# A four-stage graph network: one normalisation written with a stride-zero tensor operand, and the turn of the gated layers' state one step later

## The reference

```
layer 0 (attention and feed-forward, inner part)
  scores = sum(q[src] * k[dst]) / sqrt(16) + edge_attr @ eW + eb
  attn   = softmax of the scores over the edges of one dst
  out    = segment_sum(v[src] * attn, dst) @ oW + ob
  x1     = layer_norm(x + out) * g1 + b1
  h      = gelu(layer_norm(x1 @ f1W + f1b) * gf + bf) @ f2W + f2b
  return layer_norm(x1 + h) * g2 + b2
layer 1: mean of the neighbours, two 128x128 products, L2 norm
layer 2: h = x @ lin_w.T + lin_b; three times
  agg = segment_sum((h @ weight[i])[src], dst)
  r = sigmoid(W_ir agg + W_hr h + b);  z = sigmoid(W_iz agg + W_hz h + b)
  n = tanh(W_in agg + b_in + r * (W_hn h + b_hn))
  h = (1 - z) * n + z * h
layer 3: concat(x, mean of the neighbours) @ weight
```

## Time and profile before

| what | us |
|---|---|
| median of the runs (3) | 6054.59 |
| lowest and highest run | 6049.87, 6078.45 |
| profiled execution | 6070.21 |
| its span | 6068.3 |

### The profile page before, as it was taken

How to read it: one execution, slowest core, us unless ns; L and a number is a source line. 1 busy time by engine, 2 the same in 40 slices (tenths; PEclk the granted TensorE clock), 3 DMA queues, 4 the chain that set the end, 5 groups by cost and what they waited for, 6 DMA issues and landing times. The chain is left out here.

```text
span 6068.3 us, 76920 instructions
## 1 busy us (share of the span) xinstructions
PE 4367.1 (72%) x16790; PEld 2619.4 (43%) x16790; DVE 4101.2 (68%) x13622; ACT 2768.2 (46%) x6238; POOL 3623.7 (60%) x3234
## 2 busy tenths in 40 slices
PE   6688859999998565545666579977896669936643
PEld 3355544444444333334444344534443334436643
DVE  6566658999998544447776576557665889836633
ACT  0233326777776010136666345534443446536643
POOL 4665638888886788845555661046204757855455
PEclk8787769999999777778888899989998889968876
DMA  6222223333332343356665575457544667757621
GB/s 213 62 76 72 73 66 88 99 100 98 98 98 75 74 62 62 59 102 198 187 199 181 169 210 161 131 150 216 172 141 141 176 161 204 202 163 226 190 78 54
DMA packets 767746, 802.51 MB, mean 132 GB/s; under 512 B 139776, under 2 KB 527944, under 8 KB 767162
## 3 DMA queue, kind: packets, MB, share of 16 engines
q1 hardware_dynamic: 405498, 393.44, 22.9%
q0 software_dynamic: 117504, 209.42, 14.6%
q10 hardware_dynamic: 244288, 194.72, 9.6%
HBM read 445.32 MB, written 351.92 MB: 131 GB/s over the span
## 5 line engine op out<-in xcount | busy, mean ns | idle before, releaser
L462 PE MATMUL gate_bank<-gate_ht,gate_whh 128*128 128x512 f32 x1764 | 872.4, 618 | 28.6 <-DVE gate_n L532 15.8
L925 POOL DMA_INDIRECT xh<-mean_xh,mean_pos_all x392 | 378.4, 965 | 338.9 <-DVE mean_xh L1027 142.2
L462 PEld LDWEIGHTS gate_bank<-gate_ht,gate_whh 128*128 128x128 f32 x1764 | 341.8, 202 | 407.0 <-issue 384.7
L2080 PE MATMUL back_ps_sums<-back_same,back_rows 128*128 128x512 f32 x400 | 286.6, 883 | 291.5 <-DMA back_rows<-x_a,back_idx 291.5
L151 POOL DMA_INDIRECT ffn_rows<-att_sums,ffn_idx x392 | 409.6, 1045 | 114.8 <-issue 106.3
L289 POOL DMA_INDIRECT gate_rows<-h_a,by_pos x200 | 197.8, 989 | 429.0 <-POOLq L117 328.4
L1521 PE MATMUL ffn_ps_f<-ffn_hg,ffn_f 128*128 128x512 f32 x784 | 407.1, 616 | 47.6 <-ACT ffn_hg L1698 47.6
L458 PE MATMUL gate_bank<-by_rank,gate_win 128*128 128x512 f32 x882 | 436.0, 594 | 0.0
L1514 PE MATMUL ffn_ps_u<-ffn_xs_t,ffn_up_w 128*128 128x512 f32 x784 | 387.0, 596 | 1.1 <-issue 1.1
L2061 POOL DMA_INDIRECT back<-back_out,back_dest x200 | 324.1, 1620 | 67.8 <-issue 60.1
L583 ACT ACTIVATE gate_z<-gate_bank,gate_b_rz 128x512 f32<-128x512 f32 x294 | 201.5, 685 | 346.0 <-PE gate_bank L462 225.6
(11 more groups left out here) (273 smaller groups left out, 12080.1 us busy)
## 6 DMA issues: line engine op xcount, KB each, us to landing
mean_x<-x_a SPq DMA_DIRECT2D x196, 256.0 KB
back<-blank ACTq DMA_DIRECT2D x99, 264.0 KB, 4.5
mean_rows<-back SPq DMA_DIRECT2D x98, 264.0 KB
hp<-mean_xh SPq DMA_DIRECT2D x98, 264.0 KB
gate_x<-xh SPq DMA_DIRECT2D x98, 264.0 KB
gate_hot<-hot_rows SPq DMA_DIRECT2D x100, 256.0 KB
ffn_x<-in_x_in SPq DMA_DIRECT2D x98, 256.0 KB
ffn_xr<-in_x_in SPq DMA_DIRECT2D x98, 256.0 KB
```

The source lines that it names most:

```text
L462: last = nc.tensor.matmul(bank_[:, :], whh[:, c * D:(c + 1) * D], ht[:, t.slot4, :], start=not inputs, stop=True)
L925: nc.gpsimd.indirect_dma_start(out=g["xh"][:, :], out_offset=bass.IndirectOffsetOnAxis(ap=pos_all[:, t.n, j:j + 1], axis=0), in_=xh[:, t.n ...
L2080: last = nc.tensor.matmul(ps_sums[t.slot][:, :], rows[:, t.slot4, j, :], same[:, t.slot, j, :], start=j == 0, stop=j == J - 1)
```

## The change

In the feed-forward, L1615 becomes a scalar_tensor_tensor: the mean stays a value for each partition, and inv becomes a tensor operand of 128x128 whose stride is zero, so that each partition reads its one value 128 times. In the gated layers, the turn L484 and what follows it (copy or addition, statistics, power, apply, stores, the load of x_c, the scatter) stand one step later, the guards of hn and of its stores allow four items instead of two, and hn and ht_stored have four slots. The loops of PE and ACT run one step longer in all three layers, those of the other engines in layer 2. Left out below: hunks that only change the length of a loop, and unchanged lines.

```diff
@@ -362,7 +362,7 @@
         r, z, n1, n3 = (f.sb(s, [P, 2, SUPER]) for s in ("r", "z", "n1", "n3"))
-        d, hn = (f.sb(s, [P, 2, SUPER]) for s in ("d", "hn"))
+        d, hn = f.sb("d", [P, 2, SUPER]), f.sb("hn", [P, 4, SUPER])
         outs = 6 if final else 2
@@ -370,7 +370,7 @@
         ht_loaded = f.sems("ht_loaded", 4)
-        stored, ht_stored = f.sems("stored"), f.sems("ht_stored")
+        stored, ht_stored = f.sems("stored"), f.sems("ht_stored", 4)
         r_made, z_made, nh_made, ni_made, h_turned = (
@@ -413,12 +413,12 @@
                     sums.store_hots(sp, e)
-                if final and (t := item_at(5)) and t.has:
+                if final and (t := item_at(6)) and t.has:
                     wait(sp, stored[t.m % 2], 16 * (t.m // 2 + 1))
...
                                  ).then_inc(back_loaded[t.m % 4], 16)
-            over_items(5 if final else 0, step)
+            over_items(6 if final else 0, step)
             if initial:
@@ -429,11 +429,11 @@
             def step(edges_at, item_at):
-                if final and (t := item_at(5)):
+                if final and (t := item_at(6)):
                     ln.rstd(nc, pool, t, y_done)
...
                     sums.gather(pool, e)
-                if final and (t := item_at(6)) and t.has:
+                if final and (t := item_at(7)) and t.has:
                     wait(pool, ids_made, 1)
@@ -477,12 +477,12 @@
                     gate(ps_z, 1, t, z_made, True, t.has)
-                if t := item_at(2):
+                if t := item_at(3):
                     wait(pe, h_done, t.n + 1)
...
                         last = nc.tensor.transpose(ps_out[:, j * D:(j + 1) * D],
-                                                   hn[:, t.slot, j * P:(j + 1) * P], g["ident"][:, :])
+                                                   hn[:, t.slot4, j * P:(j + 1) * P], g["ident"][:, :])
                     last.then_inc(h_turned, 1)
@@ -519,10 +519,10 @@
                     wait(dve, d2_done, t.n + 1)
-                    wait(dve, h_turned, t.n - 1)
+                    wait(dve, h_turned, t.n - 3)
                     if not final:
-                        wait(dve, ht_stored[t.slot], 16 * t.u)
-                    nc.vector.tensor_tensor(hn[:, t.slot, :], d[:, t.slot, :], n3[:, t.slot, :],
+                        wait(dve, ht_stored[t.slot4], 16 * t.u4)
+                    nc.vector.tensor_tensor(hn[:, t.slot4, :], d[:, t.slot, :], n3[:, t.slot, :],
                                             ALU.add).then_inc(h_done, 1)
@@ -531,9 +531,9 @@
                                                    ALU.add, ALU.mult).then_inc(n1_done, 1)
-                if final and (t := item_at(5)):
+                if final and (t := item_at(6)):
                     ln.shifts(nc, dve, t, y_done)
-                if final and (t := item_at(2)):
+                if final and (t := item_at(3)):
                     wait(dve, h_turned, t.n + 1)
@@ -570,19 +570,19 @@
                                          ).then_inc(id_done, 1)
-                if final and (t := item_at(6)):
+                if final and (t := item_at(7)):
                     wait(act, stored[t.slot], 16 * t.u)
...
                              [y[:, t.slot, j, :] for j in range(J)], y_done)
-                if not final and (t := item_at(2)):
+                if not final and (t := item_at(3)):
                     wait(act, h_done, t.n + 1)
-                    act.dma_start(ht_out[t.tile], hn[:, t.slot, :]).then_inc(ht_stored[t.slot], 16)
+                    act.dma_start(ht_out[t.tile], hn[:, t.slot4, :]).then_inc(ht_stored[t.slot4], 16)
                 if t := item_at(1):
...
                                          bias=b_rz[:, 1:2]).then_inc(z_done, 1)
-                if not final and (t := item_at(2)):
+                if not final and (t := item_at(3)):
                     wait(act, h_turned, t.n + 1)
@@ -593,21 +593,22 @@
                                          bias=b_ih[:, 2:3]).then_inc(n_done, 1)
-                if not final and (t := item_at(2)):
+                if not final and (t := item_at(3)):
                     wait(act, out_done, t.n + 1)
...
                     nc.scalar.activation(ht[:, t.slot4, :], ps_in[:, :], ACT.Copy).then_inc(ht_made, 1)
-                if final and (t := item_at(6)):
+                if final and (t := item_at(7)):
                     wait(act, y_done, t.n + 1)
                     act.dma_start(part_tile(x_out, t.tile, 0, D), y[:, t.slot, :, :]).then_inc(stored[t.slot], 16)
-            over_items(6 if final else 2, step)
+            over_items(7 if final else 3, step)
             for b in range(2):
                 act.wait_ge(stored[b], 16 * (NT // 2))
-                if not final:
-                    act.wait_ge(ht_stored[b], 16 * (NT // 2))
+            if not final:
+                for b in range(4):
+                    act.wait_ge(ht_stored[b], 16 * ((NT - b + 3) // 4))
 
@@ -1612,9 +1613,9 @@
                     for j in range(J):
-                        last = nc.vector.tensor_scalar(xh[:, t.slot4, j, :], a[:, t.slot4, j, :],
-                                                       mv[:, root_slot(t, LN1), LN1, j, 0:1], inverse(t, LN1)[:, j:j + 1],
-                                                       ALU.subtract, ALU.mult)
+                        last = nc.vector.scalar_tensor_tensor(
+                            xh[:, t.slot4, j, :], a[:, t.slot4, j, :], mv[:, root_slot(t, LN1), LN1, j, 0:1],
+                            inverse(t, LN1)[:, j:j + 1].broadcast_to([P, D]), ALU.subtract, ALU.mult)
                     last.then_inc(xh_done, 1)
...
                     wait(dve, roots_done, roots_by(t, LN3))
```

More of the change, by code:

```diff
@@ L444, in step @@
                             in_=back_x[:, t.m % 4, j, :], in_offset=None).then_inc(back_scattered[t.m % 4], 16)
-            over_items(6, step)
+            over_items(7 if final else 0, step)
             if final:
@@ L498, in step @@
                     sums.sum(pe, e)
-            over_items(2, step)
+            over_items(3, step)
         @block.vector
@@ L556, in step @@
                     nc.vector.tensor_copy(g["node_at"][:, HT:NT, :], g["tails"][:, HT:NT, :, 0]).then_inc(ids_made, 1)
-            over_items(5 if final else 2, step)
+            over_items(6 if final else 2, step)
         @block.scalar
```

## The result

Thirteen runs of each kernel on the same chip: before 6063.07 us (median), changed 6034.46 us; the ratio is 0.9947 (95% interval 0.9934 to 0.996), so 32 us faster (24 to 40; the two medians lie 28.6 apart). The forecast was 12 us faster, 6043 us, with a range of 6025 to 6060 us: the time lies in the range and the sign is right, but the forecast difference is less than half of the measured one. A ratio of 0.9947 is also just outside the 0.5% that the forecast called "same", on the side to which it gave a chance of 0.24.

What follows compares the result with a forecast made beforehand. POOL was taken to bound the feed-forward, with other engines or transfers bounding the gated stretches. Feed-forward -11, layer 2 first half -4, second half +3, rest 0: -12 us from 6054.6, so 6043 us, range 6025 to 6060.

Steps and rivals of the forecast that it cites:

- POOL bounds, DVE's stall is no loss: Feed-forward: POOL's list takes 10.75 us a tile; DVE waits inside L1615 and has 2.0 us of slack a tile.
- Rival 1: Feed-forward normalisation: the zero-stride operand doesn't hold the shared port, gathers run undisturbed, -37 us there, 6017 us; chance 0.12.
- Rival 2: Feed-forward: DVE's normalisation gets in between L1469 and L1474 and delays POOL, +24 us, 6078 us; chance 0.12.
- Rival 4: Feed-forward: the second gather misses its gap between the L1630 again, +14 instead of -11 us, 6068 us; chance 0.10.
- The feed-forward term: POOL's second gather loses 0.06 to 0.18 us less, 0.13 taken, in 85 tiles: -11 us.
- the pitch: Feed-forward: new normalisation instructions follow each other at 0.285 us instead of 0.25, moving the L1630 later.
- the rule of the gap: Feed-forward: a gather waits for the DVE instruction under way, about 0.15 us into its own time, then gets in.
- Layer 2's first half: DVE bounds its 48 steps of 7.42 us; its wait for the turns in L540 goes: -4 us.
- First scatter: Layer 2, second half: DVE's variance comes one step later and the whole chain of scatters with it: +5.7 us.
- the chain of scatters: Layer 2, second half: earlier steps give back 1.0 us, and POOL waits less for DVE in 6 tiles, -1.8 us.
- Layers 0 and 1: Gated layers held by PE, DVE's additions or transfers, not the turns: 0, with +1 us at most at their ends.
- Rival 3: First half of layer 1: the turns were holding it, -30 us there, 6013 us; chance 0.08.

Runs made afterwards that it cites:

- slack: Changed kernel with DVE's L1608 done twice per feed-forward tile, the extra one ahead of the normalisation; tile 10.554 us, 0.9956 of before.
- stt_late: Changed kernel with the shift L1623 done twice per tile, so that the L1631 stand 0.07 us later; 0.9999 of before.
- ts_late: Kernel before, tensor-scalar kept, with the shift L1622 done twice per tile, so that the L1630 stand 0.07 us later; 1.0016 of before.
- ffn_only: Kernel before with only the rewritten feed-forward instruction, gated layers unchanged; 0.9972 of before.
- gated_only: Kernel before with only the gated-layer part of the diff, feed-forward unchanged; 0.9989 of before.
- xb_dve: Changed kernel with POOL's feed-forward addition L1475 (ffn_xb) done by DVE at the end of its step; 1.0071 of before.
- both_dve: Changed kernel with both POOL additions of the feed-forward, L1470 (ffn_a) and L1475 (ffn_xb), done by DVE; 0.9938 of before.

## Why the prediction was right, and where it was off

**POOL bounds, DVE's stall is no loss: right.** slack put 0.66 us into it for nothing. Rival 1 (the lock is gone) is out by the maximum of 2579 ns, although its sign, a start other than 0.2 us behind L1469, did come (0.48): DVE reaches the normalisation later, but still before POOL's pair is through. Rival 2 (DVE gets in between) is out by L1475, whose median is 1.26 us and whose longest is 1.32. Rival 4 (the gap is missed) is out for the changed kernel, and is what stt_late does.

**The feed-forward term: sign and place (POOL's gathers, the second) right, reason wrong, size near by luck.** Forecast were 0 for the first gather and -0.06 to -0.18 for the second; measured +0.07 and -0.25, together -0.18 a tile and -15 us for -11. The term rested on two numbers. One was the pitch: 0.285 for the new instruction, from 1.13 us for four; but a group's time holds the tail of its last one, and the starts in the timelines are 0.262 apart, against 0.256 for tensor-scalar. So three pitches give 0.02 and not 0.09; what moved the L1630 was that the first new instruction ends 0.15 us behind POOL's pair and not 0.09. The total shift behind the pair is 0.09, just below the forecast's 0.10 to 0.22. And the second gather moved as well, by the 0.07 that the first one lost, which the forecast had at nothing ("stays at some 0.12 lost"): against it the last L1630 moved only from 0.096 to 0.109 us. The other number was the rule of the gap, 0.15 us into the gather's own time. By it and by these distances the gather misses the gap in both kernels, and by it ts_late had to be faster: it is refuted. That this term came out near its forecast is luck.

**Layer 2's first half, -4 forecast, -12 measured: the term mis-sized.** The mechanism is the one named, DVE's wait for the turns in L540. The size was read from the waits view, which leaves out short idle times, and in most steps the delay was 0.10 us: 9.5 and not 4.2. Some 2.3 us more are only the second step, which lacks an L540 now (5.08 us instead of 7.42) and is paid at the end of the half. The forecast itself had named a gated half changed by over 10 us as a sign of being wrong, and this half changed by 12.2.

**First scatter, +5.7 forecast, +9.7 measured: the step that failed.** I moved POOL's power and had the scatter follow it. That L419 moves too was in the list of what the edit moves, and I didn't price it: L419 stands in SP's queue behind loads that wait for L540, so it went two steps later, and it, not the variance, is what the scatter waits for. By ffn_only's 0.2 us it was so before the change already. It gave back 4.0 us more in the first pair of profiles (2.4 in gated_only, where the scatter starts 34.1 us behind that L532 and in ffn_only 26.0); the chain of scatters then ran 4.7 us shorter instead of the 2.8 forecast (1.0 and 1.8). Layer 2 in all: -7.1 instead of -1.

**The sum.** Of -12 us, the stretches gave -22 and the runs -32. The time fell into the range because the range was 35 us wide, not because the terms were sized right.

**Layers 0 and 1: nothing, as forecast.** Rival 3 is out by gated_only, whose first half of layer 1 takes 248.4 us, and ffn_only's 249.2.

The Trainium skill's rule (SBUF — State Buffer, Who interferes with whom), that a VectorE instruction with two SBUF inputs contends with a GpSimd one that reads SBUF: the trace agrees again, the new form stands for 1.9 us behind POOL's pair. Its inference, that such an instruction does not hold the making of descriptors: the trace differs in so far as a gather takes 0.95 us beside statistics and up to 1.35 beside L1630. A gather also reads its indices (ffn_idx) from SBUF, and which of its two parts is held the trace doesn't tell.

## What to carry to other kernels

An engine that stalls inside an instruction looks busy and is not the bound: sum the other engine's list and see whether it has waits. Where GpSimd issues gathers beside two-operand VectorE instructions, a shift of these by 0.07 us changed one gather by 0.06 to 0.29 us (later made it longer and earlier shorter, in all four kernels); no formula here forecast the size, so try the orders. A waits view leaves out short idle times, which add up over many steps: compare the starts of successive lines as well. And price a moved step in every queue that carries its transfers: both the failed term of the forecast and the failed xb_dve were loads held in SP's queue behind another wait. Taking such waits away, with the additions on DVE, gave more than the change itself.

## What the hardware showed unexpectedly

- A gather beside statistics instructions (one tensor from SBUF) takes 0.947 us. The first of a tile's four takes 1.02 even with statistics alone beside it, and also in both_dve, where POOL does no addition.
- POOL's power (2.94 us) did not hold two-operand additions of DVE: in both_dve 81 of the 98 ffn_a additions ran wholly beside one and none took over 0.72 us. POOL's own addition L1470 held 32 of 98 in xb_dve, although it started up to 0.65 us behind them.
- A 128x128 scalar-tensor-tensor with a stride-zero tensor operand runs at a pitch of 0.262 to 0.263 us, the same as with a full one, and 0.006 to 0.007 above tensor-scalar.
- The same kernel took some 500 us less on three other chips (mean granted clock 0.90 to 0.91 against 0.865), all of it outside the feed-forward, layer 0's second half and layer 2.
